# A delta-rule stage whose triangular inverse is built from 64-wide quadrants and a merge

## The reference

```python
def step(Sm, inp):
    q_, k_, v_, g_, b_ = inp
    Sm = Sm * jnp.exp(g_)[..., None, None]
    kv = jnp.einsum('bhk,bhkv->bhv', k_, Sm)
    delta = (v_ - kv) * b_[..., None]
    Sm = Sm + jnp.einsum('bhk,bhv->bhkv', k_, delta)
    o = jnp.einsum('bhk,bhkv->bhv', q_, Sm)
    return (Sm, o)
_, o = jax.lax.scan(step, S0, (qt, kt, vt, gt, bt))
```

## Time and profile before

| what | value |
|---|---|
| device time, median of 3 runs | 6041.69 us (6040.69 to 6044.21) |
| the profiled execution's span | 6046.2 us |
| the 64 stages | 233.5 to 3361 us |
| busy over the span: PE, PEld | 5221.5 us (86%), 3893.8 us (64%) |
| busy over the span: DVE, ACT, POOL | 3480.2 us (58%), 3055.8 us (51%), 1178.3 us (19%) |

### The profile page before, as it was taken

The page is one execution under the profiler, slowest core; times in us unless marked ns, Lnnn a source line. Parts: engine busy times, 40 slices in busy tenths (PEclk is TensorE's granted clock), DMA queues, the critical chain, the costliest instruction groups (busy, mean ns, idle before and its releaser), DMA issues. The chain is left out here.

```text
span 6046.2 us, 91895 instructions
## 1 busy us (share of the span) xinstructions
PE 5221.5 (86%) x32318; PEld 3893.8 (64%) x32318; DVE 3480.2 (58%) x6531; ACT 3055.8 (51%) x8923; POOL 1178.3 (19%) x1352
## 2 busy tenths in 40 slices
PE   5799999999989999989999699899998597399969
PEld 4477777877877778877887555555555354255545
DVE  3466666676666667666766566555552554543331
ACT  2466666666656666666666344344441244325421
POOL 0222222322222222222232100011110321002210
PEclk7799999999999999999999799899999798688879
DMA  2000000000000000000000100100000100000000
GB/s 85 19 19 17 13 19 19 18 17 17 19 19 13 17 19 19 17 14 19 22 19 13 46 1 1 65 1 0 0 0 20 27 1 13 21 1 1 1 21 14
DMA packets 51094, 103.57 MB, mean 17 GB/s; under 512 B 12848, under 2 KB 20176, under 8 KB 49520
## 3 DMA queue, kind: packets, MB, share of 16 engines
q1 hardware_dynamic: 50672, 98.07, 5.4%
HBM read 90.43 MB, written 5.52 MB: 16 GB/s over the span
## 5 line engine op out<-in xcount | busy, mean ns | idle before, releaser
L896 ACT ACTIVATE dh_pb<-bank 64x128 f32<-64x128 f32 x3072 | 831.4, 271 | 272.5 <-PE bank L670 239.3
L684 PE MATMUL bank<-dh_cw,dh_pb 128*128 128x128 f32 x5120 | 701.5, 281 | 113.0 <-ACT dh_pb L896 111.4
L684 PEld LDWEIGHTS bank<-dh_cw,dh_pb 128*128 128x128 f32 x5120 | 635.5, 193 | 191.1 <-ACT dh_pb L896 164.4
L1034 DVE SCALAR_TENSOR_TENSOR dh_kq<-bank,dh_conv_kq,dh_kq 128x511 f32<-128x511 f32 (+2 forms) x408 | 305.4, 749 | 184.8 <-ACT dh_kq L853 173.6
L902 ACT ACTIVATE dh_cw<-bank 128x256 f32<-128x256 f32 x640 | 244.9, 385 | 255.1 <-PE bank L684 247.9
L621 PE MATMUL bank<-hT,dh_w_kq 128*128 128x512 f32 x544 | 276.7, 633 | 83.2 <-DVE dh_kq L1034 75.3
L1034 DVE SCALAR_TENSOR_TENSOR dh_v<-bank,dh_conv_v,dh_v 128x511 f32<-128x511 f32 (+2 forms) x384 | 284.2, 747 | 91.3 <-ACT dh_v L853 82.2
L1797 PE MATMUL bank<-moe_h_split,moe_w 128*128 128x512 bf16 x1200 | 277.1, 381 | 14.6 <-PEq L89 14.6
L633 PE MATMUL bank<-dh_w_vz,hT 128*128 128x256 f32 x1024 | 245.5, 383 | 22.0 <-ACT dh_zs L864 22.0
L1128 DVE TENSOR_TENSOR dh_zz<-dh_zz,bank 128x512 f32<-128x512 f32 x130 | 89.2, 686 | 283.0 <-PE bank L597 281.1
L621 PE MATMUL bank<-hT,dh_w_vz 128*128 128x512 f32 x512 | 242.5, 596 | 8.6 <-DVE dh_v L1034 8.6
(11 more groups left out here) (416 smaller groups left out, 12170.8 us busy)
## 6 DMA issues: line engine op xcount, KB each, us to landing
dh_rates<-delta_rates SPq DMA_DIRECT2D x130, 256.0 KB, 3.6
dh_w_vz<-in_L_wvz SPq DMA_DIRECT2D x17, 512.0 KB, 3.3
mod_w<-in_L_wmod SPq DMA_DIRECT2D x4, 1536.0 KB, 7.0
dh_w_kq<-in_L_wkq SPq DMA_DIRECT2D x18, 256.0 KB, 2.6
dh_wo<-in_L_wo SPq DMA_DIRECT2D x16, 256.0 KB, 4.2
moe_w<-in_L_w13T SPq DMA_DIRECT2D x1, 3200.0 KB, 15.7
later_gates<-mod_gate SPq DMA_DIRECT2D x3, 1024.0 KB, 4.0
gate<-later_gates SPq DMA_DIRECT2D x6, 512.0 KB, 3.4
```

What stands on the lines that cost most here:

```text
L684: last = pe.matmul(square(j)[:, b, :, :], pb[j][:, b, :], src[:, :, b, :], start=True, stop=True)
L896: last = act.activation(out[half, :, o, half], src[halves[o], :, half], ACT.Copy)
L1034: dve.scalar_tensor_tensor(y, pj_bank(n)[:, 0:S - i], taps(n)[:, TAPS - 1 - i:TAPS - i], y, ALU.mult, ALU.add).then_inc(s["v_cs" if i < TA ...
```

## The change

The diagonal blocks are now inverted with products of 64x64x64, each in a quadrant of the array, instead of 128x128x128 products with a block diagonal tile. C is kept whole (`ci`, 128 wide), its transpose `ct` is made once per head (`turn_c`, `c_copy`). A level computes for each head three kinds of product: the power (POW), the transposed power (TPOW) and the running inverse (INV). The results of row group g go to bank g (`lvl[0]`, `lvl[1]`), which both heads share in turn. ScalarE copies the first of these banks (`level_copy`), VectorE the second (`level_take`), GpSimd adds the identity to the transposed power (`plus`), which the next level's INV products wait for. After level 5 `last_copy` writes the diagonal blocks into `ttb`, and two more steps (`cross`, `corner`) compute the block beside the diagonal of the inverse itself, so that `z_prod` applies the full inverse at once: `w_prod`, `x_prod`, `w_copy`, `zeta`, `off_diagonal`, `grow` and `inverse` are gone. The order of all four engines' lists is new; on VectorE `decay` now stands between `level_take` 4 of head 0 and of head 1, and `qk_mask` behind `start_power`; on GpSimd `gated_out` has moved from the front of a = 1 into the middle.

```diff
-    def turn_power(pe, t, i, j):
-        ...
-    def square_power(pe, t, i, j):
-        ...
+    def first_level(pe, t, j):
+        h = hs[j]
+        pe.wait_ge(h["a_ct"], t + 1)
+        if j == 0:
+            after(pe, s["a_y"], t)
+        else:
+            pe.wait_ge(hs[0]["a_lv"], 5 * t + 1)
+            pe.wait_ge(hs[0]["v_lv"], 5 * t + 1)
+        ...
+    def level(pe, t, i, j):
+        h = hs[j]
+        pe.wait_ge(h["a_lv"], 5 * t + i)
+        pe.wait_ge(h["v_lv"], 5 * t + i)
+        if j == 0:
+            pe.wait_ge(hs[1]["a_lv"], 5 * t + i)
+            pe.wait_ge(hs[1]["v_lv"], 5 * t + i)
+        elif i < 5:
+            pe.wait_ge(hs[0]["a_lv"], 5 * t + i + 1)
+            pe.wait_ge(hs[0]["v_lv"], 5 * t + i + 1)
+        else:
+            pe.wait_ge(hs[0]["a_x"], t + 1)
+        for kind in (POW, TPOW, INV):
+            if kind == INV:
+                pe.wait_ge(h["p_qi"], 5 * t + i)
+            if i == 4 and kind == POW or i == 5 and kind != INV:
+                continue
+            for sl in range(2):
+                for g in range(2):
+                    for o in range(2):
+                        w = lv[halves[g], j, g ^ o, sl, :, :]
+                        lhs = (w[:, TPOW, :], w[:, POW, :], qi[j][halves[g], g ^ o, sl, :])[kind]
+                        last = pe.matmul(lvl[g][halves[g ^ o], sl, kind, :], lhs, w[:, kind, :], start=True, stop=True)
+        if i == 5:
+            for sl in range(2):
+                for o in range(2):
+                    last = pe.matmul(lvl[o][halves[o], sl, POW, :], lv[halves[o], j, 0, sl, INV, :],
+                                     qi[j][halves[o], 0, sl, :], start=True, stop=True)
+        last.then_inc(h["t_lv"], 1)
+    def cross(pe, t):
+        for j in HEADS: pe.wait_ge(hs[j]["a_x"], t + 1)
+        ...
+    def corner(pe, t):
+        pe.wait_ge(s["a_g"], t + 1)
+        ...
     def tensor_stage(pe, t):
...
+        turn_c(pe, t, 0)
+        v_turn(pe, t, 0)
+        if old:
+            for j in HEADS: ks(pe, t, j)
+        turn_c(pe, t, 1)
+        v_turn(pe, t, 1)
+        side_tensor(pe, q, a, 0)
+        z_prod(pe, t, 0)
+        first_level(pe, t, 0)
+        z_prod(pe, t, 1)
+        if old: qs(pe, t, 0)
+        first_level(pe, t, 1)
+        side_tensor(pe, q, a, 1)
+        pu(pe, t, 0)
+        level(pe, t, 1, 0)
+        ...
+        level(pe, t, 4, 0)
+        qk_prod(pe, t)
+        level(pe, t, 4, 1)
+        side_tensor(pe, q, a, 9)
+        for j in HEADS: y_turn(pe, t, j)
+        level(pe, t, 5, 0)
+        w_out(pe, t, 0)
+        level(pe, t, 5, 1)
+        w_out(pe, t, 1)
+        cross(pe, t)
+        corner(pe, t)
...
+    def level_copy(act, t, i, j):
+        act.wait_ge(hs[j]["t_lv"], 6 * t + i + 1)
+        kinds = slice(TPOW if i == 4 else POW, INV + 1)
+        act.activation(lv[:, j, 0, :, kinds, :], lvl[0][:, :, kinds, :], ACT.Copy).then_inc(hs[j]["a_lv"], 1)
+    def last_copy(act, t, j):
+        act.wait_ge(hs[j]["t_lv"], 6 * t + 6)
+        act.wait_ge(hs[j]["t_z"], t + 1)
+        for g in range(2):
+            out = ttb[halves[g], j, :, halves[g]]
+            act.activation(evens(out), lvl[g][halves[g], :, INV, :], ACT.Copy)
+            act.activation(odds(out), lvl[1 - g][halves[g], :, INV, :], ACT.Copy)
+            last = act.activation(t1[halves[g], j, :, :], lvl[g][halves[g], :, POW, :], ACT.Copy)
+        last.then_inc(hs[j]["a_x"], 1)
...
+    def level_take(dve, t, i, j):
+        dve.wait_ge(hs[j]["t_lv"], 6 * t + i + 1)
+        kinds = slice(TPOW if i == 4 else POW, INV + 1)
+        dve.tensor_copy(lv[:, j, 1, :, kinds, :], lvl[1][:, :, kinds, :]).then_inc(hs[j]["v_lv"], 1)
...
     def vector_stage(dve, t):
...
+        level_take(dve, t, 4, 0)
+        for j in HEADS: decay(dve, t, j)
+        level_take(dve, t, 4, 1)
+        if a == 2: key_vectors(dve, q)
+        if a == 3: query_vectors(dve, q)
         for j in HEADS: normed(dve, t, j)
-        for j in HEADS: grow(dve, t, 5, j)
+        for j in HEADS: start_power(dve, t, j)
         qk_mask(dve, t)
-        for j in HEADS: decay(dve, t, j)
-        for j in HEADS: start_power(dve, t, j)
-        inverse(dve, t, 0)
         collect(dve, t)
-        inverse(dve, t, 1)
...
+    def plus(pool, t, i, j):
+        h = hs[j]
+        pool.wait_ge(h["a_lv"], 5 * t + i)
+        pool.wait_ge(h["v_lv"], 5 * t + i)
+        pool.tensor_tensor(qi[j][:, :, :, :].rearrange("p r s n -> p (r s) n"),
+                           lv[:, j, :, :, :, :].rearrange("p r s k n -> p (r s) k n")[:, :, TPOW, :], mask_bc(ids[:, :], NB),
+                           ALU.add).then_inc(h["p_qi"], 1)
...
     def pool_stage(pool, t, kh):
-        if a == 1: gated_out(pool, q)
         if a == 2: next_gates(pool, q, kh + q + 1)
         for j in HEADS: injected(pool, t, j)
         if a == 3: value_scale(pool, q)
-        for j in HEADS: off_diagonal(pool, t, j)
+        plus(pool, t, 1, 0)
         if inner: faded(pool, t, 0)
         scores(pool, t, 0)
+        plus(pool, t, 1, 1)
         if inner: faded(pool, t, 1)
+        plus(pool, t, 2, 0)
         scores(pool, t, 1)
+        plus(pool, t, 2, 1)
+        if a == 1: gated_out(pool, q)
+        for j in HEADS: plus(pool, t, 3, j)
         rms(pool, t)
+        for i in (4, 5):
+            for j in HEADS: plus(pool, t, i, j)
```

More of the change, by code:

```diff
@@ L660, in qk_prod, with turn_c @@
         each(pe, B_AUX, lambda b: key(par, c, b), lambda b: query(par, c, b)).then_inc(s["t_qk"], 1)
-    def turn_power(pe, t, i, j):
+    def turn_c(pe, t, j):
+        after(pe, hs[j]["v_u"], t)
+        if j == 0:
+            after(pe, s["a_g"], t)
+        else:
+            pe.wait_ge(hs[0]["a_ct"], t + 1)
+        each_turned(pe, TURN, lambda b: ci[j][:, b, :]).then_inc(hs[j]["t_tr"], 1)
+    def first_level(pe, t, j):
         h = hs[j]
-        if i:
-            pe.wait_ge(h["a_c"], 5 * t + i)
-        else:
[L667 to L673, removed]
@@ new lines, in first_level @@
+        for kind in (POW, TPOW, INV):
+            for sl in range(2):
+                for more in range(2 if kind == INV else 1):
+                    for g in range(2):
+                        for o in range(2):
+                            c = ci[j][halves[g], 2 * sl + o, halves[g]]
+                            cT = ct[j][halves[g], 2 * sl + o, halves[g]]
+                            one = ids[halves[g], :]
+                            lhs, rhs = ((cT, c), (c, cT), (one if more else cT, one))[kind]
+                            last = pe.matmul(lvl[g][halves[g ^ o], sl, kind, :], lhs, rhs, start=(more == 0),
+                                             stop=(kind != INV or more == 1), skip_group_check=True)
@@ new lines, in scalar_stage @@
+        level_copy(act, t, 2, 0)
+        mean_sq(act, t, 0)
+        side_silu(act, q, a, 2)
+        side_scalar(act, q, a, 4)
+        level_copy(act, t, 2, 1)
+        mean_sq(act, t, 1)
+        side_silu(act, q, a, 3)
+        side_scalar(act, q, a, 5)
+        level_copy(act, t, 3, 0)
+        side_silu(act, q, a, 4)
+        side_scalar(act, q, a, 6)
+        level_copy(act, t, 3, 1)
+        side_silu(act, q, a, 5)
+        side_scalar(act, q, a, 7)
+        side_scalar(act, q, a, 8)
+        level_copy(act, t, 4, 0)
@@ L1027, in convolve @@
+        side_silu(act, q, a, 6)
+        level_copy(act, t, 4, 1)
+        side_scalar(act, q, a, 9)
+        for j in HEADS: y_copy(act, t, j)
+        last_copy(act, t, 0)
+        side_silu(act, q, a, 7)
+        last_copy(act, t, 1)
+        cross_copy(act, t)
+        corner_copy(act, t)
     def convolve(dve, q, n):
@@ L1481, in _ @@
         def _(dve):
-            for f in (rhs, zeta, q_state, output, normed):
+            for f in (rhs, q_state, output, normed):
                 for j in HEADS: f(dve, 0, j)
```

434 lines of the change are left out of this document (141 added, 293 removed).

## The result

The changed kernel takes 6184.33 us (median of 4 runs, 6174.54 to 6200.60) beside 6042.95 us (6040.69 to 6050.23) for the kernel before: ratio 1.0233, 95% interval 1.0216 to 1.0250, slower. The profiled execution has a span of 6181.9 us, 135.7 more than before. The 64 stages hold all of it: from the first `v_turn` to that of the epilogue they average 51.01 us after and 48.88 before, 64 x 2.13 = 136 us.

What follows compares the result with a forecast made beforehand. TensorE bounds by load, but its saving is waited away behind VectorE: four stages 191.8 plus 6.8 for the clock against 193.6, +80 us over 16 groups, less 3.6 in the epilogue, giving 6118 us; range 5960 to 6290.

Steps and rivals of the forecast that it cites:

- The sign: Whole kernel: slower, 1.3%, with chances of 0.63 slower, 0.08 same and 0.29 faster.
- the mechanism: Stage tail: TensorE waits behind VectorE's list, nearly its whole 23 us saving per four stages, then runs `w_out` at lower clock.
- TensorE's load: TensorE per stage: loses 16.9 us, gains 0.9 transposes, 7.8 quadrant products four at a time, 2.5 switches; net 5.7 less.
- C: Rival, tiled blocks: quadrants slower than four at a time; half speed gives 6370 us, one at a time over 7000; chance 0.07.
- The tail: Stage end behind the level 4 take: VectorE 7.8 us, then `w_out` to `corner`; some 14.2 us in a = 0.
- The clock's price: First `w_out` at 1.2 GHz after idle TensorE, in nearly every stage: 1.7 us a stage, 6.8 per four stages.
- Rival A: Tail without the clock's price, TensorE's work filling it enough: 6009 us, or 5910 without GpSimd's contention too; chance 0.24.
- the sum: Four stages: 191.8 + 6.8 = 198.6 us, 5.0 more than 193.6; over 16 such groups +80 us.
- Rival D: Layout missed waits from GpSimd's queue order (`plus` behind `scores` or `rms`): 1 to 3 us a stage, 6180 to 6300; chance 0.21.
- The layout: Stages laid out by the new lists: a = 0 to 3 end at 51.7, 50.9, 49.3 and 39.9 us before the clock's price.
- The epilogue's saving: Epilogue: loses the w and x products, 32 instructions, 3.6 us.
- Rival B: TensorE's load decides, VectorE runs ahead and waits stay as before: 365 us off, 5675 us; chance 0.06.

Runs made afterwards that it cites:

- fastest kernel: Changed kernel with ScalarE copying both banks, VectorE's `decay` late, and the last convolution of a = 0 stages moved behind `qk_mask`: 5676.39 us, ratio 0.9399.
- filler kernel: Changed kernel plus unused products, two ahead of `y_turn` and one ahead of `w_out` of head 0: 6109.77 us, ratio 1.0116.
- both halves of the copies: Changed kernel with ScalarE copying both banks of every level and VectorE none: 5910.16 us, ratio 0.9784.
- either half: Changed kernel with ScalarE copying both banks of level 4 only (6050.61 us, 1.0016), or of levels 0 to 3 only (6119.25 us, 1.0133).
- late-`decay` kernel: Changed kernel with VectorE's two `decay` scans moved behind `normed` and `qk_mask`: 5935.79 us, ratio 0.9817.
- kernel with `injected` late: Changed kernel with GpSimd's `injected` of both heads moved behind its next `plus`: 6114.32 us, ratio 1.0121.

## Why the prediction came out as it did

The sign, the place and the mechanism were right; the forecast of the profiled execution, 6122 us, was 60 us short of 6181.9, 0.9 us a stage.

**TensorE's load.** Right in form: level 1 of one head in the changed kernel,

```profile
448.68 0.69 PE L723 MATMUL bank<-dh_lv 64*64 64x64 f32 x32
449.20 0.41 PE L723 MATMUL bank<-dh_lv,dh_qi 64*64 64x64 f32 x16
449.54 1.16 PE L603 MATMUL bank<-dh_S,dh_kq 128*128 128x128 f32 x8
```

is 0.86 us from start to start for 48 instructions, a switch included: four at a time. That is 0.16 over the 0.7 forecast and far from the 1.3 of C, which is refuted. A group of four takes 0.058 us from start to start, where I had 0.056; the rest is the first group behind a full product (0.107 us) and the last one before the next (0.17). My reading of the earlier trace rows as a quarter of the full width was too good (0.83 us against 2.7 is three tenths), but the price of a group that I took from it held. 32 of the instructions start within 0.52 us, 16 ns each, below the 25 ns that the Trainium skill gives as the floor from start to start (TensorE: Matmul & The Clock Gate, "Wait — 56ns, not 53.3ns?"); by that floor the 32 would take 0.8. The quadrant blocks of an a = 3 stage of the fastest kernel add up to 11.2 us (forecast 7.8 + 2.5 = 10.3), and its TensorE time without idle is 4.0 us a stage below that of before (48.88 - 4.13 against 43.22 - 2.44), forecast 5.7. ScalarE's busy time fell by 7.8 us a stage (31.4 to 23.6, by the two stretches from 250 to 3360 us), some 500 us in 64 stages, forecast 490. Part of TensorE's miss is `w_out`, whose two blocks, now next to tiled ones, grew from 3.46 to 3.85 us from start to start.

**The tail.** Forecast 14.2 + 1.7 = 15.9 us behind the take in a = 0; measured 17.5 (473.3 to 490.83). VectorE's part was 8.3 us where 7.8 was forecast:

```profile
472.91 0.42 DVE L1120 COPY dh_lv<-bank 128x256 f32<-128x256 f32 x1
473.24 2.81 DVE L1097 TENSOR_TENSOR_SCAN dh_et<-dh_rates,dh_inj 128x512 f32<-128x512 f32 x2
...
476.29 1.81 DVE L1164 TENSOR_TENSOR dh_yy<-dh_yy,dh_rho 128x512 f32<-128x512 f32 x2
478.03 2.97 DVE L1106 TENSOR_TENSOR dh_c<-dh_kkm,dh_et 128x512 f32<-128x512 f32 x2
480.92 0.68 DVE L1090 TENSOR_TENSOR dh_qkm<-bank,mask_le 128x512 f32<-128x512 f32 x1
```

I had priced the contention of `plus` on `normed` and of `injected` on `start_power` (both right), but the scans at 2.3, as if alone; beside `plus` they take 2.81. TensorE's part is the larger miss, 9.2 us against 8.1:

```profile
481.75 3.75 PE L814 MATMUL bank<-dh_wo_gated,dh_ww 128*128 128x256 f32 x8 [1.41 <-DVE dh_qkm L1090]
485.43 0.71 PE L723 MATMUL bank<-dh_lv,dh_qi 64*64 64x64 f32 x16
485.91 0.64 PE L727 MATMUL bank<-dh_qi,dh_lv 64*64 64x64 f32 x8
486.48 2.64 PE L814 MATMUL bank<-dh_wo_gated,dh_ww 128*128 128x256 f32 x8
489.05 0.68 PE L738 MATMUL bank<-dh_ttb,dh_ct 64*64 64x64 f32 x16
```

The first `w_out` is 3.68 us from start to start, where I had 1.75 and 1.7 for the clock. The block between the two `w_out` is 1.05 where I had 0.55 (it takes 0.62 in the fastest kernel, at full clock), and from the second `w_out` to the stage's end it is 4.35 where my terms add up to 3.94; that `w_out` is slow in its first part too (2.57 for 1.9). The granted clock is 0.50 from 477.6 to 487.8 us, which covers the first two and the start of the third. The clock's price in a = 0 is over the 1.7 that I gave it.

**The clock.** The mechanism was right, its spread over the kinds was not: the first `w_out` takes 3.75, 1.97, 3.34 and 2.53 us (medians). a = 1 pays little (its first `w_out` is slow in 4 of 16 stages), and it alone came in under the forecast (51.5 for 52.6); a = 0 pays most. Rival A named the right point (the idle stretches of the tail) and the wrong side of it; removing the clock's price by itself gave 75 us and not the 109 of the sum. What A had for it was misread in one thing: the stages of before have a longer idle stretch than 1.4 us, 1.80 us once in each a = 1 stage, and the clock is still 1.00 over the stretch.

So two misses of opposite sign met. Without the clock's price the sum says 6009 us, and the filler kernel, at full clock, takes 6110, 101 us more; the clock's price was 34 us less than forecast. That 6118 came within 66 us of 6184 is in part luck. Rival D's band (6180 to 6300) holds the result as well, but not by the waits that it names: the trace of the changed kernel shows nothing that waits for `plus`.

**The layout.** Stages of 53.4, 52.6, 51.0 and 41.6 forecast, 55.4, 51.5, 52.7 and 43.2 measured. The take (4, 0) in a = 0 ends at 37.9 for a forecast 37.5, and the first `w_out` starts 46.3 us after `turn_c` for a forecast 45.4. The step that I read too lightly is where the tail begins: I took the take's end as given by VectorE's load, and charged the tail by its instructions. The experiments show that its order and the takes in it are worth more than any of their lengths: 249 us for the scans' place, 134 us for the two takes of level 4. The epilogue's saving of 3.6 us did not show: from the epilogue's `v_turn` to the end the changed kernel takes 2685.7 us, the one before 2683.3, and the edited ones 2678 to 2692. Rival B, TensorE's load decides, at 5675 us, is what the fastest kernel reaches (5676), but by coincidence: with a smaller saving than B had (4.0 for 5.7) and shorter waits than before (2.4 us a stage for 4.1).

What stays open: why 75 of the 274 us are had only when both halves of the copies move. Most of them lie in a = 1 and a = 3, and in a = 3 part is the clock's (the first `w_out` takes 2.85 us with either half and 1.98 with both); the rest is not shown.

## What to carry to other kernels

A copy that is given to a second engine to share the load is also a place where that engine's in-order list waits for the producer; price it by what stands behind it, not by its 0.5 us. Before a split is judged, sort the list behind each meeting point by who is waited for first: here the same instructions in another order were worth 4%. When an edit shortens the busiest engine's work, look for the new idle stretches at once, because they are paid for twice, as waiting and at the lower clock.

## What the runs showed of the hardware

- Short idle stretches of TensorE in a tail can be enough for the lower clock behind them. In the late-`decay` kernel an a = 0 stage has idle stretches of 1.32 us before level (4, 1) and 1.14 us before `y_turn`, and the granted clock is 0.50 from 459.05 to 465.87 us; the first `w_out` is slow in 13 of the 16 stages of this kind. One unused product in the second of these stretches brought the first `w_out` from 3.5 to 1.99 us, and the time down by 38 us. The length of one stretch does not settle it: the a = 1 stages of the same kernel wait 1.15 us before `y_turn` too and show the lower clock in 2 of 16, and so do the a = 1 stages of the kernel before, each with an idle stretch of 1.80 us.
- GpSimd and VectorE slow each other down: two scans take 2.33 us alone and 2.81 beside `plus`; two products of 128x512 in SBUF 1.28 alone and 2.97 beside `injected`. The GpSimd side pays too. GpSimd in the a = 0 stage whose VectorE stands above (`plus` of 128x256 takes 0.73 us alone):

```profile
473.47 1.50 POOL L1241 TENSOR_TENSOR dh_qi<-dh_lv,dh_ids 128x256 f32<-128x256 f32 x1 [2.38 <-DVE dh_lv L1120]
...
477.52 2.94 POOL L1234 TENSOR_TENSOR dh_inj<-ident,dh_R 128x512 f32<-128x512 f32 x2
```

  Both `start_power` and both `injected` lie between 477.52 and 481.00, 3.48 us; alone the two pairs take 1.28 and 2.08 us (an `injected` has a median of 1.04 us in the kernel with `injected` late), 3.36 in sum. So they take turns rather than share, and the second to start is the one that waits: the first scan, begun 0.23 us ahead of `plus`, takes its usual 1.22 us, `plus` 1.50 and the second scan 1.68. The Trainium skill says the same of a VectorE instruction with two SBUF inputs beside a GpSimd instruction that reads SBUF (SBUF — State Buffer, "SBUF: two separate sides": the pair of ports is an exclusive lock, held for the whole instruction), and the trace agrees.

- Quadrants of 64x64 run four at a time: 0.058 us from start to start for a group of four f32 instructions of 64 columns (0.52 us for 32, with a first step of 0.107 us behind a full product).
